# Selective-scan block and linear attention in fp32: the causal convolution as diagonal matrix products, and a new slot table

## The reference

```python
xz = einsum('bsd,ed->bse', xn, in_proj_w); x_in, z = split(xz, 2)
u = silu(causal depthwise convolution of x_in, 4 taps, + conv_b)
dt_r, B, C = split(einsum('bsd,ed->bse', u, x_proj_w), [64, 80])
dt = softplus(einsum('bsr,dr->bsd', dt_r, dt_proj_w) + dt_proj_b)
h = h * exp(dt * A) + (dt * u) * B          # for each step, 16 states
y = sum_n h * C + u * D
out = x + gate * einsum('bsd,ed->bse', y * silu(z), out_proj_w)
```

## Time and profile before

| what | us |
|---|---|
| median of 3 runs (lowest, highest) | 2515.31 (2513.39, 2518.91) |
| profiled execution | 2515.61 |
| its span | 2513.8 |
| scan stage in it (first scan to last) | 69 to 2018 |
| attention stage after it | 2018 to 2514 |

### The profile page before, as it was taken

The page is one execution under the profiler, slowest core; times in us unless marked ns, Lnnn a source line. Parts: engine busy times, 40 slices in busy tenths (PEclk is TensorE's granted clock), DMA queues, the critical chain, the costliest instruction groups (busy, mean ns, idle before and its releaser), DMA issues. The chain is left out here.

```text
span 2513.8 us, 29512 instructions
## 1 busy us (share of the span) xinstructions
PE 2096.4 (83%) x9536; PEld 1383.4 (55%) x9536; DVE 2097.6 (83%) x2299; ACT 1707.2 (68%) x3332; POOL 1891.8 (75%) x1175
## 2 busy tenths in 40 slices
PE   9877788778877887887778877886887889999999
PEld 3344455445444544554445444544544479988887
DVE  3988988899889998888888898889899966676666
ACT  3678676877687777777776787778655545556655
POOL 0698898889889989998998899989999832222325
PEclk9898789888998998899889898989897899999999
DMA  6510231032004110412041004110410211112113
GB/s 229 215 38 26 85 105 38 25 118 81 30 26 148 51 34 26 152 46 68 22 152 51 28 23 152 43 30 22 164 42 1 82 64 32 32 45 68 47 51 118
DMA packets 78072, 176.46 MB, mean 70 GB/s; under 512 B 7453, under 2 KB 10781, under 8 KB 77918
## 3 DMA queue, kind: packets, MB, share of 16 engines
q1 hardware_dynamic: 77918, 174.56, 20.9%
HBM read 157.23 MB, written 17.30 MB: 69 GB/s over the span
## 5 line engine op out<-in xcount | busy, mean ns | idle before, releaser
L1450 POOL TENSOR_TENSOR arena<-arena 128x1024 f32<-128x1024 f32 x512 | 1200.8, 2360 | 198.5 <-ACT arena L603 174.2
L1038 DVE TENSOR_TENSOR_SCAN arena<-ps,arena 128x512 f32<-128x512 f32 x1024 | 1233.2, 1251 | 15.4 <-POOL arena L1415 7.9
L603 ACT ACTIVATE ps<-arena 128x512 f32<-128x512 f32 x1087 | 719.5, 681 | 424.7 <-DVE arena L1038 352.6
L322 PE MATMUL ps<-keep,arena 128*128 128x128 f32 x4096 | 597.0, 297 | 299.8 <-POOL arena L1450 292.7
L322 PEld LDWEIGHTS ps<-keep,arena 128*128 128x128 f32 x4096 | 512.8, 153 | 483.5 <-POOL arena L1450 390.3
L272 PE MATMUL ps<-arena 128*128 128x512 f32 x1024 | 512.8, 649 | 44.8 <-issue 43.6
L1023 DVE TENSOR_TENSOR arena<-ps,arena 128x1024 f32<-128x1024 f32 x448 | 538.5, 1202 | 2.8 <-DMA arena<-scr_bc 1.5
L272 PEld LDWEIGHTS ps<-arena 128*128 128x128 f32 x1024 | 205.2, 211 | 277.3 <-issue 276.1
L603 ACT ACTIVATE arena<-arena 128x2 f32<-128x2 f32 (+2 forms) x599 | 229.0, 385 | 35.1 <-DMA arena<-in_x 10.9
L1397 POOL TENSOR_TENSOR arena<-arena 128x512 f32<-128x512 f32 x168 | 214.0, 1274 | 39.2 <-ACT arena L603 32.2
L312 PE MATMUL ps<-arena 128*128 128x512 f32 x512 | 235.3, 600 | 0.0
(11 more groups left out here) (148 smaller groups left out, 2811.2 us busy)
## 6 DMA issues: line engine op xcount, KB each, us to landing
arena<-scr_bc SPq DMA_DIRECT2D x128, 512.0 KB, 6.0
arena<-in_inT SPq DMA_DIRECT2D x128, 256.0 KB, 2.7
arena<-in_x SPq DMA_DIRECT2D x17, 512.0 KB, 4.1
scr_x<-arena SPq DMA_DIRECT2D x32, 256.0 KB, 2.0
arena_b<-scr_x SPq DMA_DIRECT2D x16, 512.0 KB, 3.7
arena_c<-scr_x SPq DMA_DIRECT2D x32, 256.0 KB, 2.9
out<-arena_c SPq DMA_DIRECT2D x32, 256.0 KB, 2.1
arena<-in_x SPq DMA_DIRECT2D x30, 256.0 KB, 3.6
```

The source lines that it names most:

```text
L322: last = e.matmul(YP[:, 128 * q:128 * q + 128], hb[G % R][:, i, 128 * q:128 * q + 128], ident, start=(g == 0 and i == 0 and q == 0), stop= ...
L603: return e.activation(o_, i_, f, **kw)
L1038: e.tensor_tensor_scan(H, DA[s % 4], H, h0, MUL, ADD).then_inc(v_sc)
L1450: e.tensor_tensor(H, H, Ct[:, GN * g:GN * g + GN, :], MUL).then_inc(g_w)
```

## The change

Each channel block's input product is now evicted raw into a buffer `xq` of 515 columns behind three columns of history. TensorE computes the convolution from it with four matmuls into a PSUM bank: a diagonal 128 x 128 matrix for each tap against `xq` shifted by the tap. ScalarE evicts that once, with the bias, into `u`. The taps' diagonal matrices are stored as 8 more blocks of `inT` and come through the same four weight buffers (56 more loads of 256 KB). GpSimd's tap sums are gone. More of the outer products go to GpSimd: 105 pairs instead of 64. ScalarE's softplus reads the `dt` bank for Relu before its Exp. All slots are set anew. In the first chunk the convolution is as before.

```diff
-        u[0], xnT[0], tp, wxp, xdbl[0], gbc[1], wdt = sb(8, T), sb(4, T), sb(3, T), sb(8, 128), sb(T), sb(512), sb(1024)
+        u[0], xnT[0] = sb(8, T), sb(4, T)
+        xq, _ = [sb(516) for _ in range(2)], sb(504)
...
-        AT = {"dt": 4, "soft": 7, "add": 6, "du": 7, "copy": 12, "yt": 5, "yb": 7, "yf": 8, "proj": (6, 14), "xdbl": (7, 3)}
-        XMM = {(3, 0): 0, (3, 4): 1, (4, 2): 2, (4, 8): 3, (4, 13): 4, (5, 0): 5, (5, 14): 6, (6, 7): 7}
+        AT = {"dt": 4, "soft": 6, "add": 5, "du": 8, "copy": 12, "yt": 6, "yb": 9, "yf": 13, "proj": (6, 14), "xdbl": (7, 4)}
+        XMM = {(3, 0): 0, (3, 7): 1, (3, 15): 2, (4, 6): 3, (5, 1): 4, (5, 3): 5, (5, 15): 6, (6, 1): 7}
+        XEV = {(3, 4): 0, (3, 10): 1, (4, 2): 2, (4, 11): 3, (5, 4): 4, (5, 5): 5, (6, 2): 6, (6, 5): 7}
+        CMM = {(3, 5): 0, (3, 12): 1, (4, 5): 2, (4, 13): 3, (5, 5): 4, (5, 8): 5, (6, 5): 6, (6, 11): 7}
+        CEV = {(3, 9): 0, (3, 15): 1, (4, 9): 2, (4, 15): 3, (5, 7): 4, (5, 10): 5, (6, 8): 6, (6, 15): 7}
...
-        pooled = lambda U, g: g in (1, 3) and U > 6 and U != 39 and (U % 8 in (0, 1, 2, 7) or U >= 56)
+        pooled = lambda U, g: U > 6 and U != 39 and g in ((1,), (1, 3), (1, 3), (1, 3), (1,), (0, 1, 3), (1, 3), (1, 3))[U % 8]
...
+            def conv_mm(c, i):
+                no = 8 * (c - 1) + i
+                e.wait_ge(a_xh, no + 1)
+                e.wait_ge(a_xq, no + 1)
+                P = bank(("c", c, i), (a_ue, no + 1), 128 * (c - 1) + CEV_AT[i] + 0.7)
+                W, X = win[c_no(c, i) % 4], xq[no % 2]
+                e.wait_ge(d_win[c_no(c, i) % 4], 16 * (c_no(c, i) // 4 + 1))
+                for w in range(4):
+                    last = e.matmul(P, W[:, w, :], X[:, w:w + T], start=(w == 0), stop=(w == 3))
+                last.then_inc(p_w)
...
+                act(X[:, 0:3], hist[:, i, 0:3] if c % 4 else zero3[:, 0:3], ACT.Identity).then_inc(a_xh)
                 e.wait_ge(p_w, x_no(c, i) + 1)
+                act(X[:, 3:T + 3], P, ACT.Identity).then_inc(a_xq)
...
+            def conv_evac(c, i):
+                e.wait_ge(p_w, c_no(c, i) + 1)
...
-                act(u[c % 2][:, i, :], P, ACT.Identity, bias=col("conv_b", i), scale=col("conv_w", 4 * i + 3))
...
-                for w in (2, 1, 0):
...
-                    act(tp[:, w, 0:k], old[:, w:3], ACT.Identity, scale=col("conv_w", 4 * i + w)).then_inc(a_xh)
-                    act(tp[:, w, k:T], P[:, 0:T - k], ACT.Identity, scale=col("conv_w", 4 * i + w)).then_inc(a_tp)
...
+                act(u[c % 2][:, i, :], BG[bank_of["c", c, i]], ACT.Identity, bias=col("conv_b", i)).then_inc(a_ue)
...
-            def tap(c, i, w):
-                v, no = u[c % 2][:, i, :], 8 * (c - 1) + i
-                e.wait_ge(a_tp, 3 * no + 3 - w)
-                if w < 2:
-                    e.wait_ge(g_tap, 3 * no + 2 - w)
-                e.tensor_tensor(v, v, tp[:, w, :], ADD).then_inc(g_tap)
...
+    taps = np.zeros((8, 128, 4, 128), np.float32)
+    taps[:, range(128), :, range(128)] = a["conv_w"].reshape(8, 128, 4).transpose(1, 0, 2)
```

More of the change, by code:

```diff
@@ L133, in program @@
             ("ft", "q", "v", "k", "qt", "kt", "kv", "ya", "o"))
-        a_sc, a_A, a_row, a_no, a_xn, a_xh, a_hi, a_tp, a_e0, a_du, a_su, a_xd, a_abs, a_ex, a_ln, a_sz, a_da, a_st, a_dg, a_x1, a_sm, a_sq, a_rl = (
-            sem("a_" + n) for n in ("sc", "A", "row", "no", "xn", "xh", "hist", "tp", "e0", "du", "su", "xd", "abs", "ex", "ln", "sz",
+        a_sc, a_A, a_row, a_no, a_xn, a_xh, a_hi, a_e0, a_xq, a_ue, a_du, a_su, a_xd, a_abs, a_ex, a_ln, a_sz, a_da, a_st, a_dg, a_x1, a_sm, a_sq, a_rl = (
+            sem("a_" + n) for n in ("sc", "A", "row", "no", "xn", "xh", "hist", "e0", "xq", "ue", "du", "su", "xd", "abs", "ex", "ln", "sz",
                                     "da", "st", "dg", "x1", "sm", "sq", "rl"))
@@ L145, in program @@
                                     "att", "y", "o"))
-        g_c, g_r1, g_r2, g_r3, g_rs, g_nm, g_tap, g_dt, g_du, g_gw, g_w = (sem("g_" + n) for n in ("c", "r1", "r2", "r3", "rs", "nm", "tap", "dt", "du", "gw", "w"))
+        g_c, g_r1, g_r2, g_r3, g_rs, g_nm, g_dt, g_du, g_gw, g_w = (sem("g_" + n) for n in ("c", "r1", "r2", "r3", "rs", "nm", "dt", "du", "gw", "w"))
         g_att, g_m1, g_mask, g_l1, g_l2, g_lrs, g_q, g_xo = (sem("g_" + n) for n in ("att", "m1", "mask", "l1", "l2", "lrs", "q", "xo"))
@@ L159, in program @@
[L159 to L170, removed]
@@ L199, in program @@
                     WSEQ.append((c + 1, XMM[j, pr]))
+                if (j, pr) in CMM and c + 1 < NCH:
+                    WSEQ.append((c + 1, 16 + CMM[j, pr]))
                 if (j, pr) in ZMM and U + ZMM[j, pr] < NU:
@@ L205, in program @@
         z_no = lambda U: w_no[U // 8, 8 + U % 8]
+        c_no = lambda c, i: w_no[c, 16 + i]
         kept = lambda U: U // 8 % 4 < 3
@@ L215, in program @@
         tail_of = lambda U, pr: ([TAILM[U, pr]] if (U, pr) in TAILM else []) + TAILX.get((U, pr), [])
-        XEV_AT, OUT_AT = ({i: 16 * k[0] + k[1] for k, i in D.items()} for D in (XEV, OUTA))
+        XEV_AT, CEV_AT, OUT_AT = ({i: 16 * k[0] + k[1] for k, i in D.items()} for D in (XEV, CEV, OUTA))
         NEV_AT = {2 * (U // 8 + 1) + i: 16 * U + pr for (U, pr), i in NEV.items()}
@@ L283, in x_mm @@
                 else:
-                    last = (a_tp, 24 * (c - 1) + 3 * i + 3)
-                in_proj(c, x_no(c, i), bank(("x", c, i), last, 128 * (c - 1) + XEV_AT[i] + 2 if c else None))
+                    last = (a_xq, 8 * (c - 1) + i + 1)
+                in_proj(c, x_no(c, i), bank(("x", c, i), last, 128 * (c - 1) + XEV_AT[i] + 0.7 if c else None))
+            def conv_mm(c, i):
[8 more added lines that the diff above has]
+                last.then_inc(p_w)
             def z_mm(U):
@@ L389, in _ @@
                         z_mm(Z0[pr])
+                    if more and (j, pr) in XMM:
+                        x_mm(c + 1, XMM[j, pr])
+                    if more and (j, pr) in CMM:
+                        conv_mm(c + 1, CMM[j, pr])
                     if (j, pr) in ZMM and U + ZMM[j, pr] < NU:
                         z_mm(U + ZMM[j, pr])
-                    if more and (j, pr) in XMM:
-                        x_mm(c + 1, XMM[j, pr])
                     if more and (j, pr) == AT["proj"]:
@@ L806, in _ @@
                     x_evac(c + 1, XEV[j, pr])
+                if more and (j, pr) in CEV:
+                    conv_evac(c + 1, CEV[j, pr])
                 if more and (j, pr) == AT["xdbl"]:
@@ L823, in _ @@
                     silu = True
-                if (j, pr) in ZSILU:
+                if U > 0 and (j, pr) in ZSILU:
                     for d in ZSILU[j, pr]:
@@ L1433, in _ @@
                     du(U + 1)
-                if more and (j, pr) in TAP:
-                    tap(c + 1, *TAP[j, pr])
                 if s in EXP:
@@ L1625, in _ @@
                     used += 1
+                if (j, pr) in CMM and more:
+                    used += 1
                 if (j, pr) in ZMM and U + ZMM[j, pr] < NU:
@@ L1752 @@
         "rows": np.stack([a["ada_b"][1024:1536], g["bq"], g["bv"], g["b_out"]]),
-        "inT": a["in_proj_w"].reshape(16, 128, 4, 128).transpose(0, 3, 2, 1),
+        "inT": np.concatenate([a["in_proj_w"].reshape(16, 128, 4, 128).transpose(0, 3, 2, 1), taps]),
         "xpT": np.concatenate([a["x_proj_w"][0:64], zero32, a["x_proj_w"][64:96]]).T,
```

52 lines of the change are left out of this document (29 added, 23 removed).

## The result

| what | us |
|---|---|
| before, median of 4 runs | 2514.43 (2513.39 to 2518.91) |
| changed, median of 4 runs | 2315.8 (2315.35 to 2317.51) |
| ratio, 95% interval | 0.9208, 0.9192 to 0.9224 |
| predicted, own range, range | 2343, 2310 to 2385, 2298 to 2425 |

The kernel is 199 us faster. The page of the changed kernel has the busy times (answering to the earlier trace rows) and the groups that answer to the earlier trace rows. Its lines are shifted: L1460 is GpSimd's product with C, L1057 the scans, L1042 and L1427 the outer products on VectorE and GpSimd, L301 the diagonal products, L329 the output products.

A forecast was written before the change was run, and what follows sets the result against it. VectorE was taken to bound the scan stage, idle mainly for `y_back`: 2515.6 - 171 - 46 + 49 + 3 = 2350.6, less about half of 16 us of other waits, gives 2343 us; own range 2310 to 2385, 8 in 10 2298 to 2425.

The forecast's parts named there:

- the likeliest case: The forecast itself for the whole kernel: 2343 us, own range 2310 to 2385, chance 0.58.
- The wait for `y_back`: VectorE before its final products: later slots remove 171 of 181 us; bounds 181 or nothing.
- The reading of unit 27: Scan stage: `y_back` comes a few us late because TensorE works its queue in order; VectorE waits about 3 us a unit.
- the engines behind it are not short of time: Scan stage: claim that the late chain before the final product, 181.0 us of waits, is no lack of engine time.
- The pairs: Outer products: 41 more pairs on GpSimd, 1.12 us saved each, take 46 us off VectorE.
- TensorE: Third chunk: TensorE needs 208 us with the diagonal products, between 202 at best and 234 at worst.
- 52 us of new waits: VectorE's queue: 5 us a chunk for TensorE's lag, 2 for 1.2 GHz, 49 in seven chunks, 3 for the last.
- Half given back: Rival: the wait returns before the outer products as TensorE and GpSimd fill, 140 us; 2439 us, chance 0.17.
- TensorE becomes the bound: Rival: in units 3 to 6 TensorE exceeds VectorE by 50 us a chunk; 2639 us, chance 0.08.
- The other waits: VectorE before scans and outer products: about half of 16 us goes, through ScalarE's shorter bursts and fewer GpSimd stalls.
- which no term has: Sign of being wrong: VectorE waiting for ScalarE, for which the forecast had no term.
- The clock: TensorE in a chunk: clock 0.93 or more expected; by the skill's bank-cycling rule it would stay near 234 us.

The follow-up runs named there:

- experiment 5: Changed kernel with the copy of the sums back at slot 5, `y_back` at 7, final product at 8: 2461.5 us, 0.9789.
- experiment 1: Kernel before with only the final product moved from slot 8 to slot 11 of the next unit: 2416.5 us, 0.9604.
- experiment 4: Changed kernel with the old 64 pairs on GpSimd instead of 105: 2343.6 us, 0.9316.
- experiment 9: Kernel before with the final product at slot 11 and each GpSimd tap sum cut to 2 of 512 columns: 2366.0 us, 0.9387.
- experiment 10: Kernel before, final product at slot 11, tap sums and ScalarE's three scaled copies cut to 2 columns: 2358.4 us, 0.9361.
- experiments 2 and 3: Kernel before with 105 instead of 64 pairs on GpSimd: 2567.4 us; the same with the final product also at slot 11: 2501.3 us.
- experiment 6: Changed kernel with one of the four diagonal products, the other three taps left out: 2296.8 us, 0.9133.
- experiment 7: Changed kernel with the diagonal products done twice, 224 matmuls more: 2508.9 us, 0.9973.

## Why the prediction was right

The forecast was 2343 us, the time 2315.8: the likeliest case, in its own range, 27 us too high. Step by step:

*The wait for `y_back`:* 171 us predicted to go, 179.7 went (181.0 less 1.3). The reading of unit 27 held: a late chain, cured by slack. What it left open is who kept the bank closed to TensorE for 2.74 us there. ScalarE's timeline of the kernel before answers it:

```profile
903.69 0.76 ACT L603 ACTIVATE arena<-ps,keep 128x512 f32<-128x512 f32 x1
...
906.62 0.17 ACT L603 ACTIVATE arena<-ps 128x3 f32<-128x3 f32 x1
```

Between these rows stand the convolution's three shifted copies out of ps7, and TensorE's next product may enter that bank only after the last copy (906.05 + 0.68 = 906.73); it starts at 906.89. So the old convolution's evictions held the bank for 3 us, and the change makes one full copy of them. How much of the 181 us that alone was is not shown: experiment 5 has the short eviction and still waits 186.8 us, and no run has the short one at the old slots of the kernel before.

One sentence of the reading didn't hold: I wrote that "the engines behind it are not short of time". With the tap sums kept, the move alone brings 97 us (experiment 1), since 70 us of waits came back elsewhere. The step was sound only together with the relief of GpSimd, which I had costed at nothing. Of the 73 us between experiments 1 and 4, 50 to 55 are GpSimd's time in the sums (experiment 9), about 8 the copies (experiment 10), and the other 10 to 15 the new slots and what is left of the small operations, less what TensorE's products cost; these were not separated.

*The pairs:* 46 us predicted, and VectorE's busy time did fall by 47.9. In time they are worth 28 (experiment 4), since 14 us of it come back as waits. They would be a loss in the kernel before (experiments 2 and 3).

*TensorE:* 208 us a chunk predicted from bounds of 202 and 234; measured 205.5, and 29.77 us where six products lie between two `y_back`, as counted (29.8). I charged 52 us of new waits, and this is the term that was mis-sized: VectorE's waits outside the final product rose from about 18 us to 39, and taking three quarters of the products away gains 19 us (experiment 6). That is 2.7 us a chunk, where I had put 5 for its falling behind by 7.2 and 2 for a stretch at 1.2 GHz. "Half given back" and "TensorE becomes the bound" would have needed 20 and 32 us a chunk; the doubled products reach 28 (experiment 7), with 147.8 us of waits before the outer products, so the mechanism of "half given back" exists, one convolution further on.

*The other waits:* I let the 16 us before the scans and outer products fall by half, for the end of GpSimd's stalls and ScalarE's shorter bursts. Those for GpSimd fell from 7.9 to 2.4 us, but those for ScalarE rose from 7.4 to 13.8, which is the sign that I had named as one of being wrong, "which no term has". It is small and it stays without an explanation.

*The clock:* 0.96 to 0.97 in the chunks against 0.89 to 0.91; from 795 to 900 us TensorE is busy all the time at 2.4 GHz, with two PSUM banks changing hands. Before, the slow product came after TensorE had stood idle for 2.74 us, and such gaps are rarer now. What the Trainium skill's page "TensorE: Matmul & The Clock Gate" says in the section "A second HAM failure mode: psum-queue depth-cycling", is told of a bf16 kernel: its cycling through banks, with short idle times between groups, makes the clock swing. The forecast was right not to follow it to 234 us: 49 tenants share the two banks in each chunk, and the clock is higher than with 41. What went with the clock here was TensorE's idle time, which had become less (last section).

*The sum:* the waits for `y_back` fell by 180 us, VectorE's busy time by 48, its other waits in the stage rose by 21, and its first wait behind the stage by 6: 2515.6 - 180 - 48 + 21 + 6 is 2315, against 2315.6 for the profiled execution. The forecast of 2343 misses it by one term: the waits for TensorE's sums grew by 21.5 us (1.3 to 22.8), not by 52, which is 30 us. Its smaller errors nearly cancel, and that is luck: 9 us more from the move and 2 more from the pairs, against 7 for the other waits that did not go and 6 behind the stage, which no term has.

## What to carry to other kernels

A wait that came back in every unit, while no engine was busy all the time, was a chain that is late. Slack cured it, but only as far as the other engines had room for the faster pace, so sum the work of all of them before and after. Here the edits depended on each other: the move alone gains 97 us, the pairs alone lose 53, the two without the convolution's change gain 13, and all together gain 199. And where several engines are busy for nearly all of a stage, test the edge by adding work (27 us a chunk more cost all of the 27): that the first convolution was nearly hidden said nothing of the second.

## What was unexpected of the hardware

Adding 201.6 us of products raised TensorE's busy time by only 51.4 us. The pairs' sums took 439.0 us in chunks 2 to 7 before and 402.1 after, at equal counts, and the input products 386.9 and 349.5:

```profile
L322 PE MATMUL ps<-keep,arena 128*128 128x128 f32 x3072 | 439.0, 293 | 225.7 <-POOL arena L1450 222.8 <-ACT arena L603 2.7
L272 PE MATMUL ps<-arena 128*128 128x512 f32 x768 | 386.9, 651 | 36.5 <-issue 36.5
```

```profile
L339 PE MATMUL ps<-keep,arena 128*128 128x128 f32 x3072 | 402.1, 281 | 46.6 <-POOL arena L1460 43.8 <-ACT arena L622 2.7
L278 PE MATMUL ps<-arena 128*128 128x512 f32 x768 | 349.5, 599 | 13.1 <-issue 13.1
```

The first fence is of the kernel before, the second of the changed one. Idle time of TensorE is what stood before its slower stretches. In the fourth chunk of the kernel before each of the ten falls of the clock lies in or just behind an idle time of 1.2 to 3.5 us: seven of these are waits for GpSimd's product in front of a sum, two stand before an input product ("issue"), one is for ScalarE. The three falls in the changed kernel's fourth chunk lie the same way. Not every idle time is followed by one: at 959.18 TensorE starts again after 1.88 us, with the clock at 1.00 before and after. The waits for GpSimd fell from 222.8 to 43.8 us, and with them the time at 1.2 GHz. So work added to an engine with such idle times was paid in part by the clock: 201.6 us of products for 51.4 us of busy time.
